# A two-layer decoder kernel: the mixture of experts computed for each row's two chosen experts instead of all eight

## The reference, cut to what matters

```python
x = x + _L0_attn_ref(_layernorm(x), ...)            # stage A
x = x + _L0_xattn_ref(ctx, ctx, _layernorm(x), ...) # stage B
x = x + _L0_ffn_ref(_layernorm(x), gate_w, w1, w2, w3)
x = x + _L1_attn_ref(_layernorm(x), ...)            # stage D
x = x + _L1_xattn_ref(_layernorm(x), ctx_1024)
x = x + _L1_ffn_ref(_layernorm(x), ...)

def _L0_ffn_ref(hidden_states, gate_w, w1, w2, w3):   # E=8, H=128, F=512
    logits = x @ gate_w
    mult, sel = _sparse_mixer_routing(logits)          # two experts and their factors per row
    w = jnp.sum(mult[:, :, None] * (sel[:, :, None] == jnp.arange(E)), axis=1)
    h = jax.nn.silu(jnp.einsum('th,ehf->etf', x, w1)) * jnp.einsum('th,ehf->etf', x, w3)
    return jnp.einsum('etf,efh,te->th', h, w2, w)
```

## Time and profile before

| | |
|---|---|
| times of three runs | 471.93, 472.18, 473.66 us; median 472.18 |
| span of the profiled execution | 471.6 us, 0.6 below that median; no other time of that execution is given |
| TensorE busy | 444.0 us, 94% |
| VectorE, ScalarE, GpSimd busy | 311.1, 234.4, 193.7 us |
| mean granted TensorE clock | 0.989 |
| moved by DMA | 10.78 MB, nearly all in the first 36 us |

### The profile page before, as it was taken

One profiled execution on the slowest core, in us unless ns is written; L12 is line 12 of the kernel. 1 busy time (PEld: TensorE's weight loads), 2 busy tenths in 40 slices (PEclk: granted clock), 3 DMA queues, 4 the chain that ended last, 5 costly groups with the idle time before them and its releaser, 6 DMA issues.

```text
span 471.6 us, 8631 instructions
## 1 busy us (share of the span) xinstructions
PE 444.0 (94%) x2815; PEld 344.3 (73%) x2815; DVE 311.1 (66%) x940; ACT 234.4 (50%) x678; POOL 193.7 (41%) x256
## 2 busy tenths in 40 slices
PE   0999999999999999999999999999999989797998
PEld 0457677867888878878788888888888767384554
DVE  4888787678473775744866463766336796868673
ACT  1235464644666555664564565464555723834030
POOL 4562023301456637653346344645544451404030
PEclk9999999999999999999999999999999979999899
DMA  8940000000000000000000000000000000000000
GB/s 294 383 149 1 1 1 1 0 2 2 2 0 2 1 1 0 2 1 2 1 1 1 2 0 1 1 3 1 0 2 1 1 0 13 0 13 2 0 13 11
DMA packets 10172, 10.78 MB, mean 23 GB/s; under 512 B 528, under 2 KB 7824, under 8 KB 10000
## 3 DMA queue, kind: packets, MB, share of 16 engines
q1 hardware_dynamic: 8944, 9.18, 5.7%
q10 hardware_dynamic: 1184, 1.05, 0.7%
HBM read 9.71 MB, written 0.52 MB: 22 GB/s over the span
## 4 chain that ended last, share of the span: by engine, by line
PE 73%; DVE 11%; issue 8%; ACT 4%; POOL 2%; DMA 2%; SPq 0%; DVEq 0%; ACTq 0%; POOLq 0%
PE FU L783 12%; PE FU L570 11%; PE FU L572 10%; PE AC L580 9%; PE Op L672 8%; PE Sp L648 3%; PE Tp L699 2%; PE Tp L658 2%; PE Sp L624 2%; PE Sp L628 2%; PE Sp L621 2%; PE Sp L646 2%; DMA text<-in_ctx 2%; PE Mp L777 1%; ACT kbd L868 1%
## 5 line engine op out<-in xcount | busy, mean ns | idle before, releaser
L475 POOL TENSOR_TENSOR hh<-hh,uu 128x256 f32<-128x256 f32 x128 | 93.3, 733 | 103.4 <-DVE hh L1229 102.5
L1229 DVE SCALAR_TENSOR_TENSOR hh<-th,FU 128x256 f32<-128x256 f32 x128 | 53.6, 420 | 69.8 <-ACT uu L800 57.0
L783 PE MATMUL FU<-causal_b,identb 128*128 128x512 bf16 x373 | 93.7, 388 | 0.0
L570 PE MATMUL FU<-xallT,w1s 128*128 128x256 f32 x256 | 80.0, 394 | 4.4 <-DVE hh L1229 4.1
L810 ACT ACTIVATE th<-FU 128x256 f32<-128x256 f32 x128 | 49.3, 385 | 67.0 <-PE FU L572 64.6
L580 PE MATMUL AC<-hh,w2s 128*128 128x256 f32 x256 | 77.8, 386 | 0.0
L572 PE MATMUL FU<-xwT,w3s 128*128 128x256 f32 x256 | 76.6, 381 | 0.0
L469 POOL TENSOR_TENSOR rstd<-powed,minus_half 128x1 f32<-128x1 f32 (+1 forms) x36 | 22.1, 614 | 103.9 <-DVE powed L999 84.7
L783 PEld LDWEIGHTS FU<-causal_b,identb 128*128 128x128 bf16 x373 | 37.3, 101 | 33.4 <-issue 2.9
L572 PEld LDWEIGHTS FU<-xwT,w3s 128*128 128x128 f32 x256 | 48.9, 191 | 6.7
L570 PEld LDWEIGHTS FU<-xallT,w1s 128*128 128x128 f32 x256 | 42.7, 192 | 13.4 <-DVE hh L1229 7.1
(11 more groups left out here) (219 smaller groups left out, 725.9 us busy)
## 6 DMA issues: line engine op xcount, KB each, us to landing
w1s<-in_w SPq DMA_DIRECT2D x8, 256.0 KB, 6.6
w3s<-in_w SPq DMA_DIRECT2D x8, 256.0 KB, 6.2
w2s<-in_w SPq DMA_DIRECT2D x8, 256.0 KB, 7.1
params<-in_params SPq DMA_DIRECT2D x1, 1626.0 KB, 10.9
consts<-in_consts ACTq DMA_DIRECT2D x1, 517.0 KB, 6.9
x<-in_x ACTq DMA_DIRECT2D x1, 512.0 KB, 4.9
text<-in_ctx SPq DMA_DIRECT2D x1, 512.0 KB, 7.5
out<-x SPq DMA_DIRECT2D x4, 128.0 KB, 1.8
```

The lines of the kernel that those rows point to most:

```text
L475: nc.gpsimd.tensor_tensor(hh[:, u % NB, :], hh[:, u % NB, :], uu[:, u % NB, :], ALU.mult)\
L570: mm(FU[:, u % 2, 0:256], w1s[:, e, c * P:c * P + P], xallT[:, q % 2, :, :].rearrange("p t n -> p (t n)"), start=True, stop=True)
L783: mm(FU[:, 0, :], identb[:, :], causal_b[:, :].unsqueeze(1).to_broadcast([P, 8, 64]), start=True, stop=True)
L1229: v.scalar_tensor_tensor(hh[:, u % NB, :], th[:, u % NB, :], 1.0, FU[:, u % 2, 0:256], ALU.add, ALU.mult)\
```

## The change

The mixture becomes a sparse one, and all eight tiles form one group (`TG = 8`, `NGRP = 1`).

- When all eight tiles have passed stage B and their gate logits lie in `base`, `route` picks two experts per row; `rank` (16 small bf16 products against ones and a triangle) gives each row its place in its experts' lists; `slots` turns that into row numbers, and into a table `tab` that says for each of 23 units (`NU`) which expert and which rows it takes; `spread` and `mults` make the return addresses and the two factors per row.
- GpSimd's `scatter` writes the rows of `xall` to a DRAM list `xg` with 16 indirect DMAs of 128 rows each. The list has been filled with zeros by one 4 MB DMA that SP issues near the start (in the place of the 24 weight transfers).
- Each of the 23 units takes 128 listed rows of one expert. SP reads a row number out of `tab` into a register and loads that expert's weights (`weights_in`, 768 KB, into one of three buffers `wbuf`; it waits for the `down` of the unit three back), reads another and loads the 128 rows (`rows_in`, 64 KB), and stores the result (`rows_out`). TensorE transposes the rows and computes in two halves: a half is four products of 128 columns in `gate_up` and two in `down`. So there are 46 halves.
- GpSimd's `gather` fetches the two results of every row with 16 more indirect DMAs once all 23 units are stored; `combine` on VectorE adds them to `x` with their factors. Stage D of a tile waits for its `combine`.
- `plan()` has SP as a fifth engine, `LANDING` times for transfers, new costs, a new `URGENCY` table and another order of `JOBS`; pieces of one name stay in their order.

The number of units is fixed: 1024 rows times two choices are 2048 row entries, and 23 units compute 2944.

```diff
+TG = 8
+NGRP = NT // TG
+REGION = TG * P
+NU = (2 * TG * P + E * (P - 1)) // P
+UNITS = NGRP * NU
+HALVES = UNITS * 2
+WROW = 3 * F
+WB = 3
...
-    "A0 A1 A2 A3 B0 B1 A4 B2 A5 B3 B4 B5 A6 D0 A7 D1 B6 B7 D2 D3 D4 D5 D6 D7").split()]
+    "A1 A2 A0 A3 A4 B2 B1 B0 A7 A5 A6 B3 B4 B7 B5 B6 D0 D1 D3 D2 D4 D5 D6 D7").split()]
...
+LANDING = {'scat': 2.5, 'gath': 2.5, 'W': 4.5, 'X': 2.0, 'Y': 2.0}
...
-        x_from = {"A": None, "B": ("update", where["A", t]), "D": ("addback", t // 2)}[L]
+        x_from = {"A": None, "B": ("update", where["A", t]), "D": ("comb", t)}[L]
...
-        add("routeA", q, "vector", 4.0, [("lgcopy", q)])
...
-        add("routeB", q, "vector", 1.2, [("zexp", q), reused])
...
-    for k in range(NQ * E):
-        add("weigh", k, "pool", 0.7, [("routeB", k // E), ("xwT", k - 2)])
...
-    for u in range(NQ * E * FC):
-        q = u // (E * FC)
-        add("gu", u, "tensor", 0.87, [("xwTin", u // FC), ("pTin", q)], f"FU{u % 2}", [("gate", u)])
-        add("uo", u, "scalar", 0.53, [("gu", u), ("h", u - NB)])
-        add("gate", u, "vector", 0.34, [("uo", u), ("down", u - NB)])
-        add("h", u, "pool", 0.7, [("gate", u)])
-        add("down", u, "tensor", 0.44, [("h", u), u % (E * FC) == 0 and ("oT", q - 1)])
...
+    for i in range(2 * NT):
+        add("scat", i, "pool", 1.0, [("slots", i // (2 * TG)), ("pnorm", i // 4)])
+        add("gath", i, "pool", 1.0, [("Y", u + i // (2 * TG) * NU) for u in range(NU)])
+    for t in range(NT):
+        add("comb", t, "vector", 0.8, [("gath", 2 * t + 1), ("gath", 2 * t), ("mults", t // TG)])
+    for u in range(UNITS):
+        g = u // NU
+        add("W", u, "sp", 0.8, [("slots", g), ("down", 2 * (u - WB) + 1)])
+        add("X", u, "sp", 0.8, [("scat", i + 2 * TG * g) for i in range(2 * TG)] + [("xgT", u - WB)])
+        add("xgT", u, "tensor", 0.15, [("X", u)], "Tp", [("xgTin", u)])
+        add("xgTin", u, "scalar", 0.3, [("xgT", u), ("gu", 2 * (u - 2) + 1)])
+        add("ysave", u, "scalar", 0.3, [("down", 2 * u + 1), ("Y", u - WB)])
+        add("Y", u, "sp", 0.8, [("ysave", u)])
+    for u in range(HALVES):
+        add("gu", u, "tensor", 0.88, [("xgTin", u // 2), ("W", u // 2)], f"FU{u % 2}", [("gate", u)])
+        add("uo", u, "scalar", 0.8, [("gu", u), ("h", u - NB)])
+        add("gate", u, "vector", 0.44, [("uo", u), ("down", u - NB)])
+        add("h", u, "pool", 0.75, [("gate", u)])
+        add("down", u, "tensor", 0.44, [("h", u), u % 2 == 0 and ("ysave", u // 2 - 1)])
...
-        w1s, w3s = sb("w1s", [P, E, F]), sb("w3s", [P, E, F])
-        w2s = sb("w2s", [P, E, FC, D])
+        wbuf = sb("wbuf", [P, WB, WROW])
...
-            for e in range(E):
-                sp.dma_start(w1s[:, e, :], d["w1"][e]).then_inc(dma_w[e], 16)
...
+            sp.wait_ge(presets, PRESETS)
+            for g in range(NGRP):
+                sp.dma_start(d["xg"][g].rearrange("(p c r) n -> p c (r n)", p=P, c=2 * TG),
+                             zeros[:, :].unsqueeze(1).to_broadcast([P, 2 * TG, 512])).then_inc(cleared, 16)
+            def weights_in(u):
+                g, j = divmod(u, NU)
+                sp.wait_ge(C["tab_ready"], g + 1)
+                if u >= WB:
+                    sp.wait_ge(C["down_mm"], 2 * (u - WB) + 2)
+                row = sp.value_load(tab[0:1, g, 0, j:j + 1], min_val=0, max_val=(E - 1) * P)
+                sp.dma_start(wbuf[:, u % WB, :], d["w"][bass.ds(row, P), :]).then_inc(w_loaded[u % WB], 16)
+            def rows_in(u):
+                g, j = divmod(u, NU)
+                sp.wait_ge(C["tab_ready"], g + 1)
+                sp.wait_ge(scattered[g], 16 * 2 * TG)
+                if u >= WB:
+                    sp.wait_ge(C["xgT_mm"], u - WB + 1)
+                row = sp.value_load(tab[0:1, g, 1, j:j + 1], min_val=0, max_val=E * REGION - P)
+                sp.dma_start(xg[:, u % WB, :], d["xg"][g][bass.ds(row, P), :]).then_inc(xg_loaded[u % WB], 16)
+            def rows_out(u):
+                g, j = divmod(u, NU)
+                sp.wait_ge(C["y_saved"], u + 1)
+                sp.dma_start(d["yg"][g][j * P:j * P + P, :], ys[:, u % WB, :]).then_inc(y_stored[u % WB], 16)
+            pieces = dict(W=weights_in, X=rows_in, Y=rows_out)
+            for stage, i in order["sp"]:
+                pieces[stage](i)
...
-            def weigh(k):
-                q, e = divmod(k, E)
-                pool.wait_ge(C["wt_ready"], q + 1)
...
-                nc.gpsimd.tensor_tensor(xw[:, k % 2, :, :], xall[:, q % 2, :, :],
-                                        wt[:, q % 2, :, e:e + 1].to_broadcast([P, 2, D]), ALU.mult).then_inc(C["xw_ready"], 1)
+            def scatter(i):
+                t, k = divmod(i, 2)
+                g = t // TG
+                pool.wait_ge(C["slot_ready"], g + 1)
+                pool.wait_ge(C["xn_ready"], t // 2 + 1)
+                pool.wait_ge(cleared, 16 * NGRP)
+                nc.gpsimd.indirect_dma_start(d["xg"][g], bass.IndirectOffsetOnAxis(slot[:, g, k, t % TG:t % TG + 1], 0),
+                                             xall[:, t, :], None).then_inc(scattered[g], 16)
+            def gather(i):
+                t, k = divmod(i, 2)
+                g = t // TG
+                pool.wait_ge(C["home_ready"], g + 1)
+                for b in range(WB):
+                    pool.wait_ge(y_stored[b], 16 * len(range(b, (g + 1) * NU, WB)))
+                nc.gpsimd.indirect_dma_start(yr[:, t, k, :], None, d["yg"][g],
+                                             bass.IndirectOffsetOnAxis(home[:, g, k, t % TG:t % TG + 1], 0))\
+                    .then_inc(gathered[t], 16)
...
+            def gate_up(v):
+                u, half = divmod(v, 2)
+                if half == 0:
+                    pe.wait_ge(w_loaded[u % WB], 16 * (u // WB + 1))
+                    pe.wait_ge(C["xgT_in"], u + 1)
+                fill(f"FU{v % 2}", (C["gated"], v + 1))
+                for part in range(2):
+                    for i in range(2):
+                        c = part * F + (2 * half + i) * P
+                        ins = mm(FU[:, v % 2, 256 * part + P * i:256 * part + P * i + P], wbuf[:, u % WB, c:c + P],
+                                 xgT[:, u % 2, :], start=True, stop=True)
+                ins.then_inc(C["gu_mm"], 1)
+            def down(v):
+                u, half = divmod(v, 2)
+                if half == 0 and u:
+                    pe.wait_ge(C["y_saved"], u)
+                pe.wait_ge(C["h_ready"], v + 1)
+                for i in range(2):
+                    c = 2 * F + (2 * half + i) * P
+                    ins = mm(AC[:, 0:P], hh[:, v % NB, P * i:P * i + P], wbuf[:, u % WB, c:c + P],
+                             start=(half == 0 and i == 0), stop=(half == 1 and i == 1))
+                ins.then_inc(C["down_mm"], 1)
...
+            def save_rows(u):
+                act.wait_ge(C["down_mm"], 2 * u + 2)
+                if u >= WB:
+                    act.wait_ge(y_stored[u % WB], 16 * (u // WB))
+                copy(ys[:, u % WB, :], AC[:, 0:P]).then_inc(C["y_saved"], 1)
...
+            def slots(g):
+                dve.wait_ge(C["rank_mm"], g + 1)
+                link(v.tensor_tensor(place[:, :, :], Mp[:, 0:TG * E].rearrange("p (t e) -> p t e", e=E),
+                                     ebase.unsqueeze(1).to_broadcast([P, TG, E]), ALU.add))
+                v.tensor_scalar(tiles_of[:, :], Mp[:, TG * E:TG * E + E], 1.0 / P, (P - 1.0) / (2 * P), ALU.mult, ALU.add)\
+                    .then_inc(C["rank_took"], 1)
+                link(v.tensor_tensor(chosen[:, :, :, :], hot[:, :, :, :], both(place[:, :, :]), ALU.mult))
+                link(v.tensor_reduce(slot_f[:, :, :], chosen[:, :, :, :], X, ALU.add))
+                v.tensor_copy(slot[:, g, :, :], slot_f[:, :, :]).then_inc(C["slot_ready"], 1)
...
+            def combine(t):
+                g = t // TG
+                dve.wait_ge(gathered[t], 32)
+                dve.wait_ge(C["mult_ready"], g + 1)
+                link(v.scalar_tensor_tensor(x[:, t, :], yr[:, t, 0, :], mult[:, g, 0, t % TG:t % TG + 1], x[:, t, :],
+                                            ALU.mult, ALU.add))
+                v.scalar_tensor_tensor(x[:, t, :], yr[:, t, 1, :], mult[:, g, 1, t % TG:t % TG + 1], x[:, t, :],
+                                       ALU.mult, ALU.add).then_inc(C["x_updated"], 1)
```

271 lines of the change are left out of this document (151 added, 120 removed).

## The result

The changed kernel took 476.16 us in the median of 20 runs (470.04 to 480.91), the kernel before 471.42 (469.79 to 473.75). The medians stand 1.0% apart; the ratio is 1.0061, with a 95% interval of 1.0033 to 1.009. Two later comparisons, on two different chips, gave 1.0001 (0.9971 to 1.0031) and 0.9932 (0.9899 to 0.9964). So by these ratios the change moves the time by less than 1%, up or down, where 450 us had been predicted. The first trace is of the longest execution (480.91 us, span 479.1), which the ratio leaves out because it counts only those within 1.5% of the fastest, and the last trace is of one of the shorter (465.38, span 463.6). The table has three traces, since they differ in more than noise.

The account below looks back on a forecast made before the run. TensorE's fixed order was taken as the kernel's clock: 191 + 28.7 + 80.5 + 12.6 + 132.5 = 445.3 us of span, 446 as median; a second sum by difference gave 452. Forecast 450 us (443 to 457), overall range 435 to 481.

Parts of the forecast that it names:

- Start to `rank`: From kernel start through the A and B jobs to `rank`: 191 us, including 12.1 idle and 72 of keep_warms.
- `rank` to the first unit: Between `rank` and the mixture's first unit: 28.7 us of TensorE work, mostly 119 keep_warms, hiding the scatter chain.
- c: GpSimd's time to issue one indirect DMA, taken as 1.2 us; the scatter chain 6.1 + 16c stays hidden up to 1.3.
- The mixture: The 23 units: 3.5 us each, 80.5 us, from a 10.1 us loop per three units and SP's 3.35 us queue.
- the second rival: In the mixture, weights come late and TensorE's clock falls to half: about 465 us, chance 0.16.
- The bound of 110 us: Upper bound for the mixture: 3 x 4.7 with slow weights and a 1.8 us register load, or SP's 2 x 1.8 + 1.35.
- the last rival: Scatters and gathers become bound by GpSimd, or the mixture by SP at register load 1.8: 480 us, chance 0.15.
- The way back: Between the mixture and stage D: 56 keep_warms, 12.6 us, barely hiding save, store and seven gathers (12.0 us).
- Stage D to the end: Stage D and the closing stages: 67 us of work, 55.4 of keep_warms, 7.9 and 2 of waits; 132.5 us.
- Late weights with the clock: In the mixture, weights taking 5 us let TensorE idle and its clock halve: about 465 us, chance 0.16.
- GpSimd's issue: Indirect DMAs at scatters and gathers: slow issue, 1.5 to 2.3 us each, 462 us (0.11); as the bound, 480 (0.15).
- The Trainium skill's rule: Behind `rank`, VectorE's two-port passes block GpSimd's descriptor writes; the chain could grow by up to 8 us, to 458.

## Why the prediction was wrong, step by step

1. **Start to `rank`**, 191: measured 193.2 to 193.5. Right; VectorE held the pace.
2. **`rank` to the first unit**, 28.7: 27.4 in the last trace. c was taken at 1.2 and is 1.26 (0.96 for the issue and 0.30 to the next), and the chain just hides. The idle time (3.8 and 2.9 us) and the half clock behind it in the first two traces were not in the sum (34.7 and 32.3).
3. **The mixture**, 80.5: measured 90.0 to 99.3. This is the step that failed. Its terms were near in the last trace: weights 4.0 (measured 4.36, for the second of three 4.45 and 5.18 in the two turns above), register load 1.0 (1.16 from the row load's issue to the weights'), products 1.8 (1.88). The loop they were put in was the wrong one: it ran through the unit's own passes on ScalarE, VectorE and GpSimd and gave 10.1 us, while TensorE's order leads it through the next unit's weights, 11.4 to 12.5 us, and 12.3 to 16.3 in the first trace, half clock included. The order was there to be read: two units' gate and up products stand in a row ahead of the first one's `down`. In the first traces the half clock comes on top (granted clock 0.91 and 0.96 over the stretch), as the second rival had it. Between the first trace and the last it is most of the difference: TensorE is busy 81.6 us in place of 73.8 with as many records, and idles 17.7 in place of 16.2.

```profile
276.68 4.57 PE L648 MATMUL FU<-xgT,wbuf 128*128 128x128 f32 x24 [1.40 <-DMA wbuf<-in_w]
```

   Here 24 records behind a wait of 1.40 us take 4.57 us at a granted clock of 0.63, where 16 take 2.05 and 24 would take 3.0. Some weights also landed later in that trace (5.98 us from 287.46 and 6.26 from 302.16 to their products); why, no run shows.

   The bound of 110 us has a slip of its own: the loop with slow weights and a register load of 1.8 adds up to 13.5 us, 4.5 per unit and not 4.7, which is 103 us. Even with 110 us the sum gives 475, not the 480 that the last rival names for it.
4. **The way back**, 12.6: 13.5 in the last trace; 2.5 us more where the copy of xnT is late.
5. **Stage D to the end**, 132.5: 135.3 to 139.2. Its waits were sized well (11.4 us idle in the last trace, 9.9 taken). The sum had no clock term; as an estimate, 0.96 over 139.2 us is 5.6 us of the miss, which no run here takes by itself.

The rivals. Late weights with the clock, 465 us at 0.16, is the nearest number below 476, 471 and 468. Its reason was half right: most weights take 4.4 us and not 5, but are asked for late. Its own sign, a clock under 0.9 in the mixture, was not met (0.91, 0.96, 1.00). GpSimd's issue is neither slow nor the bound. The Trainium skill's rule that was cited with that rival ("SBUF — State Buffer", Who interferes with whom) changes nothing visible here: the first scatter takes 1.20 us and the other 15 take 0.95 or 0.96 each, with VectorE busy beside them (until 204.0 us) and without. The Trainium skill's floor of 600 ns for a register load ("DMA: Bandwidth & Descriptors", Latency and other measured facts) is not met either; the load itself is shorter (ns, minimum/median/maximum), yet 1.16 us lie from the row load's issue to that of the weights (273.94 to 275.10, above), so the 1.0 of the sum stood for more than the load.

```profile
L494 SPq TENSOR_LOAD <-tab x23: 263/267/440, 217.1 to 300.1; - x23
```

That keep_warms and waits take most of the 120 us was named rightly; but the runs without keep_warms show that behind the mixture they mostly stand where TensorE would wait for the other engines.

## What to carry to other kernels

Where a buffer is refilled, follow the loop in the consumer's actual order: the last reader of the buffer, or what the refill's queue waits for, may stand behind work that waits for the next buffer, and then one buffer less turns than is allocated. One more buffer told this apart from a slow transfer at once (450.4 against 471.1 us, 256 against 196 GB/s). And in one in-order queue a transfer that is ready stands behind one that isn't: removing a wait pays only when what stands ahead of it in the queue is ready too (472.8 against 462.4 us).

## What the runs showed of the hardware that was not expected

- The same program, with five buffers, took 448.2 us on one chip and 442.0 on another, while the kernel before took 471.0 and 471.1. A comparison of two kernels holds for the chips that it ran on; the changed kernel stands at 1.006, 1.000 and 0.993 to the one before.
- In three of six jobs TensorE pauses 2.5 to 4.2 us in a run of narrow products around the end of GpSimd's scatters (from 211 to 217 us in the first trace, where the last scatter's issue ends at 215.7), with no semaphore as the cause, and its clock is near half behind that (0.57 and 0.58 from 215 to 223 us). Float32 products, a quarter as many and four times as long each, removed it in the one run that tried them there.
- GpSimd issues an indirect DMA of 128 rows every 1.26 us, 0.96 of it busy.
- A clock of 0.74 over stage D cost nothing that could be seen there (136.6 us, against 138.7 at 0.96 with the keep_warms): TensorE was busy for 95 of these 136.6 us and waited for the other engines in the rest.
